# Attention's start in an adaptive-layer-norm block: modulation computed as rows, gates in their own buffers, the first stack signalled by heads

## The reference

```
mod = silu(c) @ wmod                      # c: 8 x 512, wmod: 512 x 3072
sa, ca, ga, sb, cb, gb = six slices of mod, 8 x 512 each
ga, gb = sign * max(|g|, 0.25)            # sign(0) counts as +1
h = layernorm(x) * (1 + ca) + sa
x = x + ga * attention(h)                 # 16 heads of 32, causal
h = layernorm(x) * (1 + cb) + sb
x = x + gb * ffn(h)                       # 512 -> 1024 -> 1024 -> 512, relu
```

## Time and profile before

| What | us |
|---|---|
| median of 3 runs | 1556.97 |
| lowest and highest run | 1556.32, 1560.2 |
| the profiled execution | 1558.07 |
| its span in the trace | 1556.3 |
| TensorE (PE) busy | 1454.3 (93%) |
| VectorE (DVE) busy | 1110.4 (71%) |
| ScalarE (ACT) busy | 808.8 (52%) |
| GpSimd (POOL) busy | 450.3 (29%) |
| mean granted clock of TensorE | 0.97 |

### The profile page before, as it was taken

One profiled execution on the slowest core, in us unless ns is written; L12 is line 12 of the kernel. 1 busy time (PEld: TensorE's weight loads), 2 busy tenths in 40 slices (PEclk: granted clock), 3 DMA queues, 4 the chain that ended last, 5 costly groups with the idle time before them and its releaser, 6 DMA issues.

```text
span 1556.3 us, 30453 instructions
## 1 busy us (share of the span) xinstructions
PE 1454.3 (93%) x12112; PEld 1319.0 (85%) x12112; DVE 1110.4 (71%) x1953; ACT 808.8 (52%) x1462; POOL 450.3 (29%) x455
## 2 busy tenths in 40 slices
PE   7989999999999999994699999987999999999998
PEld 6678788787878888873499999987999999999998
DVE  5477878777877777672676667676676665788887
ACT  3157666667666666673355555555333333354332
POOL 2156566656576766673000000020000000000000
PEclk9889999999999999996799999998999999999999
DMA  6534444343534343434334444642665555688885
GB/s 216 162 84 123 98 97 123 89 121 80 125 82 124 90 124 82 99 77 170 134 132 153 142 143 142 230 163 82 237 227 207 210 210 184 232 279 288 304 304 183
DMA packets 126590, 247.16 MB, mean 159 GB/s; under 512 B 13672, under 2 KB 36200, under 8 KB 126448
## 3 DMA queue, kind: packets, MB, share of 16 engines
q1 hardware_dynamic: 122816, 242.57, 49.7%
q10 hardware_dynamic: 3632, 2.64, 0.5%
HBM read 114.58 MB, written 79.72 MB: 125 GB/s over the span
## 4 chain that ended last, share of the span: by engine, by line
PE 45%; DVE 4%; ACT 2%; DMA 2%; issue 1%; SPq 0%; DVEq 0%; ACTq 0%
PE sum_b L2125 11%; PE sum_e L2125 8%; PE sum_a L2125 8%; PE aux L2065 6%; PE sum_b L2121 4%; PE sum_e L2121 3%; PE sum_a L2121 3%; PE aux L2075 1%; PE aux L2053 1%; DMA y_dram<-u_c 1%; DVE op L1708 1%; DVE w L1832 1%; DMA wproj_whole<-wproj_t 1%; DVE w L1837 0%; ACT w L1493 0%
## 5 line engine op out<-in xcount | busy, mean ns | idle before, releaser
L429 POOL TENSOR_TENSOR prob_lo<-prob,prob_hi 128x512 f16<-128x512 f32 x256 | 297.2, 1166 | 138.3 <-ACT prob L533 138.0
L526 ACT ACTIVATE prob_hi<-key_score 128x512 f16<-128x512 f32 x320 | 191.2, 598 | 127.7 <-PE key_score L824 125.2
L2125 PE MATMUL sum_b<-op,w 128*128 128x256 f32 x1728 | 221.8, 287 | 12.0 <-DVE op L1708 9.7
L2125 PEld LDWEIGHTS sum_b<-op,w 128*128 128x128 f32 x1728 | 215.0, 195 | 14.8 <-DVE op L1708 7.2
L735 PE MATMUL lin<-h_parts,wqkv 128*128 128x512 f32 x768 | 218.5, 408 | 1.1 <-DVE h_parts L578 1.1
L533 ACT ACTIVATE prob<-key_score 128x512 f32<-128x512 f32 x320 | 190.6, 596 | 0.0
L697 DVE TENSOR_REDUCE row_max<-score 128x1 f32<-128x512 f32 (+2 forms) x384 | 180.4, 498 | 12.8 <-PE score L811 11.9
L735 PEld LDWEIGHTS lin<-h_parts,wqkv 128*128 128x128 f32 x768 | 143.0, 195 | 30.4 <-DVE h_parts L578 3.2
L2125 PE MATMUL sum_e<-op,w 128*128 128x256 f32 x1152 | 151.1, 289 | 5.4 <-DVE w L1832 5.4
L811 PE MATMUL score<-stack 96*128 96x512 f32 (+3 forms) x512 | 155.2, 364 | 0.0
L2125 PEld LDWEIGHTS sum_e<-op,w 128*128 128x128 f32 x1152 | 146.2, 197 | 6.4 <-DVE w L1832 5.8
(11 more groups left out here) (153 smaller groups left out, 2583.5 us busy)
## 6 DMA issues: line engine op xcount, KB each, us to landing
stack<-qk_parts SPq DMA_DIRECT2D x384, 128.0 KB, 2.4
late_op_whole<-y_dram SPq DMA_DIRECT2D x40, 512.0 KB, 4.9
y_dram<-u_c SPq DMA_DIRECT2D x32, 512.0 KB, 3.1
blk<-y_dram SPq DMA_DIRECT2D x32, 512.0 KB, 4.3
y_dram<-y_sum SPq DMA_DIRECT2D x24, 512.0 KB, 4.4
x_tiles<-x SPq DMA_DIRECT2D x32, 256.0 KB, 3.7
attn_dram<-o_rows SPq DMA_DIRECT2D x32, 256.0 KB, 2.3
attn_tiles<-attn_dram SPq DMA_DIRECT2D x8, 1024.0 KB, 6.3
```

Of the source, the lines that this page charges most:

```text
L429: nc.gpsimd.tensor_tensor(prob_lo[:, key[1] % 2, u, :], prob[:, u, :], prob_hi[:, key[1] % 2, u, :], ALU.subtract).then_inc(lo_pool, 1)
L526: nc.scalar.activation(prob_hi[:, q % 2, u, :], bank[:], ACT.Exp, scale=SOFTMAX_SCALE, bias=P_SHIFT)
L2125: mm = nc.tensor.matmul(dst, w[:, wl, c, cols], data[:, dl, c, :], start=begin, stop=end, skip_group_check=again)
```

## The change

It does the following.

- Modulation: `mod_columns(s)` no longer computes, it transposes. New `mod_row_of(s, j)` computes one of the four vectors as rows (8 x 512) by four float32 matmuls like a gate's; ACT copies the row to the new tile `mod_rows` (`take_row`), and TensorE transposes it in four pieces of 128 into `o_bank`. The two vectors of attention come ahead of the turns, their transposes after turn 1. The MLP's two are computed in slot 0, steps 1 and 3, and transposed in slot 1, step 4.
- Ahead of it TensorE runs 16 bf16 matmuls of 128x512 of the identity (`warm_up`), as soon as POOL has made identity and masks.
- Turns 2 and 3 of batch 0 use the two score banks, and `o` instead of `full`; QK 0 and QK 1 of batch 0 are interleaved piece by piece. The weights' high and low parts are put later, one piece at a time, the last two low parts into slot 0.
- Gates: they are computed in slot 1, step 2, and slot 2, step 2, with a weight tile of their own (`wm_gate`); ACT copies each to `gates`, POOL makes each by four instructions ahead of its slots 2 and 3, and SP stores them ahead of slot 3. `gates` and `sign` now share memory with stack 3, so that stack's load and its ones wait for the store; DVE's `take_gate` is gone.
- Stack 0 of batch 0 is loaded head by head, three DMAs a head, with a semaphore for each head; slots 0 and 1 wait for the head that they need.

```diff
     def load_mod(engine, i):
...
+        dst, arrived = (wm[:, half], wm_in[half]) if i < 4 else (wm_gate[:], wm_gate_in)
+        engine.dma_start(dst, wmod.rearrange("(c p) n -> p c n", p=P)[:, :, column * C:(column + 1) * C])\
+            .then_inc(arrived, 16)
+    def turn_bank_of(n, c):
+        return score_bank[c - 2] if n == 0 and c >= 2 else lin_bank_of((TURN, c))
+    def full_of(n, c):
+        return o[:, c - 2].rearrange("p t n -> p (t n)") if n == 0 and c >= 2 else full[:, c % 2, :]
...
# SP
+                if n == 0 and g == 0:
+                    sp.sem_inc(stack_in[0], 16 * STACK_DMAS)
                     for j in range(4):
+                        for block_row in range(3):
+                            load_rows(g, block_row, j, first_stack_in[j])
+                    return
+                if n == 0 and g == 3:
+                    sp.wait_ge(gates_out, 16)
+                for block_row in range(3):
+                    for j in range(4):
+                        load_rows(g, block_row, j, stack_in[g])
...
-            for step in (1, 2):
-                sp.wait_ge(mod_mm, step)
-                for half in range(2):
-                    load_mod(sp, 2 * step + half)
-                for item in before_first():
-                    if item[0] == QK and item[1] // 2 == step - 1:
-                        after_item(0, item)
+            for half in range(2):
+                sp.wait_ge(mod_mm, half + 1)
+                load_mod(sp, 2 + half)
+            load_mod(sp, 4)
+            for item in before_first():
+                after_item(0, item)
...
-                    if first and (p, u) == (1, 3):
+                    if first and (p, u) == (3, 0):
                         sp.wait_ge(gate_step, GATE_STEPS)
# POOL
+            def make_gate(g):
+                made = 4 * g
+                pool.wait_ge(gate_row, g + 1)
+                nc.gpsimd.tensor_scalar(sign[:, g], gates[:, g], 0.0, 0.5, ALU.is_ge, ALU.subtract)\
+                    .then_inc(gate_step, 1)
+                pool.wait_ge(gate_step, made + 1)
+                nc.gpsimd.tensor_tensor(gates[:, g], gates[:, g], sign[:, g], ALU.mult).then_inc(gate_step, 1)
+                pool.wait_ge(gate_step, made + 2)
+                nc.gpsimd.tensor_scalar(gates[:, g], gates[:, g], GATE_FLOOR / 2, 4.0, ALU.max, ALU.mult)\
+                    .then_inc(gate_step, 1)
+                pool.wait_ge(gate_step, made + 3)
+                nc.gpsimd.tensor_tensor(gates[:, g], gates[:, g], sign[:, g], ALU.mult).then_inc(gate_step, 1)
...
             def slot(b, p, first, more):
+                if first and p == 1:
+                    pool.wait_ge(w_lo, len(W_ORDER))
+                    pool.wait_ge(v_split, values_until(1))
+                    ones(2)
+                    pool.wait_ge(ones_ready, 4)
+                if first and p in (2, 3):
+                    make_gate(p - 2)
+                if first and p == 4:
+                    pool.wait_ge(mod_mm, 6)
+                    pool.wait_ge(gates_out, 16)
+                    pool.wait_ge(v_split, values_until(4))
+                    pool.wait_ge(lo_pool, 3 * len(LO_ON_POOL))
+                    ones(3)
+                    pool.wait_ge(ones_ready, 1 + GROUPS)
# ACT
+            def take_row(s, j):
+                act.wait_ge(mod_mm, 2 * s + j + 1)
+                nc.scalar.copy(mod_rows[:, s, j], key_bank[j][0:B, :]).then_inc(mod_row, 1)
+            def take_gate(g):
+                act.wait_ge(mod_mm, 4 + g + 1)
+                act.wait_ge(w_lo, len(W_ORDER))
+                nc.scalar.copy(gates[:, g], (key_bank[0], o_bank)[g][0:B, :]).then_inc(gate_row, 1)
+            for j in range(2):
+                take_row(0, j)
+            weights_high(0)
             for item in before_first():
                 after_item(0, item, very_first=True)
+                if item == (TURN, 1):
+                    weights_high(1)
                 if item == (TURN, NC_ - 1):
+                    weights_high(2)
+                if item == (QK, 1, NC_ - 1):
                     for k in range(3, len(W_ORDER)):
                         weights_high(k)
...
                 if first and p == 2:
-                    act.wait_ge(gates_out, 16)
+                    act.wait_ge(mod_turned, 2)
                 for u in range(UNITS):
+                    if first and p == 0 and u in (2, 4):
+                        take_row(1, u // 2 - 1)
+                    if first and (p, u) == (1, 2):
+                        take_gate(0)
+                        load_mod(act, 5)
+                    if first and (p, u) == (2, 3):
+                        take_gate(1)
# DVE
-            for k in range(3):
-                weights_low(k)
             take_columns(0)
             dve.wait_ge(mod_taken, 2)
             take_mod(0)
+            weights_low(0)
             for item in before_first():
                 after_item(0, item)
-                if item == (TURN, NC_ - 1):
-                    for k in range(3, len(W_ORDER)):
-                        weights_low(k)
-            take_columns(1)
+                if item == (TURN, 1):
+                    weights_low(1)
+                if item == (QK, 1, NC_ - 1):
+                    weights_low(2)
+            weights_low(3)
...
-                    if first and p == 1 and u in (0, 2):
-                        take_gate(u // 2)
+                    if first and p == 0 and u in (1, 3):
+                        weights_low(4 + u // 2)
+                    if first and (p, u) == (2, 0):
+                        take_columns(1)
# TensorE
+            def warm_up():
+                for _ in range(WARM_UP):
+                    nc.tensor.matmul(score_bank[0][:], ident_bf[:], ident_bf[:].unsqueeze(1).broadcast_to([P, NT, P]),
+                                     start=True, stop=True)
+            def condition_row(bank, weights):
+                for c in range(NC_):
+                    mm = nc.tensor.matmul(bank[0:B, :], silu[:, c, :], weights[:, c, :],
+                                          start=(c == 0), stop=(c == NC_ - 1))
+                mm.then_inc(mod_mm, 1)
+            def mod_row_of(s, j):
+                pe.wait_ge(wm_in[j], 16 * (s + 1))
+                if s:
+                    pe.wait_ge(mod_row, j + 1)
+                condition_row(key_bank[j], wm[:, j])
             def mod_columns(s):
                 for j in (SHIFT, SCALE):
+                    pe.wait_ge(mod_row, 2 * s + j + 1)
                     for block in range(NC_):
                         at = ((s * 2 + j) * NC_ + block) * B
+                        mm = nc.tensor.transpose(o_bank[:, at:at + B], mod_rows[:, s, j, block * P:(block + 1) * P],
+                                                 ident[0:B, 0:B])
+                mm.then_inc(mod_turned, 1)
...
+            pe.wait_ge(pool_step, 8)
+            warm_up()
             pe.wait_ge(silu_step, 3)
+            for j in (SHIFT, SCALE):
+                mod_row_of(0, j)
+            first_items = before_first()
+            first_items[NC_:3 * NC_] = [item for pair in zip(qk(0), qk(1)) for item in pair]
+            for item in first_items:
                 do_item(0, item)
+                if item == (TURN, 1):
+                    mod_columns(0)
...
+                if b == 0 and p < 2 and u in (0, 2):
+                    pe.wait_ge(first_stack_in[2 * p + u // 2], 16 * 3)
...
                 if first and p == 2:
+                    pe.wait_ge(gate_row, 1)
+                    pe.wait_ge(ones_ready, 3)
+                if first and p == 3:
+                    pe.wait_ge(gate_row, 2)
+                if first and p == 6:
                     pe.wait_ge(ones_ready, 1 + GROUPS)
                 for u in range(UNITS):
+                    if first and p == 0 and u in (1, 3):
+                        mod_row_of(1, u // 2)
+                    if first and (p, u) == (1, 2):
+                        gate_row_of(0)
+                    if first and (p, u) == (1, 4):
+                        mod_columns(1)
+                    if first and (p, u) == (2, 2):
+                        gate_row_of(1)
```

113 lines of the change are left out of this document (48 added, 65 removed).

## The result

| What | before | after |
|---|---|---|
| median of 12 runs, us | 1560.66 | 1548.63 |
| lowest and highest run | 1556.32, 1565.1 | 1546.48, 1554.56 |
| the profiled execution | 1558.07 | 1547.02 |
| its span | 1556.3 | 1545.2 |
| POOL busy | 450.3 | 465.3 |

The ratio of the runs is 0.9931 with a 95% interval of 0.9915 to 0.9946: 12 us faster, where 18.2 were forecast, and 0.13 us outside the stated range, which is less than two repeats of the same kernel differ by (1548.76 and 1548.46). Up to 75 us the times came out nearly as predicted. Slot 4 then lost 4.5 us, in the step whose cost the prediction had put at 0.5.

The account below looks back on a forecast made before the run. TensorE was taken as always busy from the fourth slot, so earlier starts reach the end whole: 17.1 before slot 0 + 1.6 in slots 0 to 2 − 0.5 for gates = 18.2 off 1558.1, stated 1540.0 us; range 1534.5 to 1548.5.

Parts of the forecast that it names:

- What bounds it: TensorE is always busy from the fourth slot, so whatever attention ends earlier should reach the end whole.
- the first row: Start up to modulation's rows: warm-up, rows and transposes let DVE take the columns at 18.7 us, 4.0 earlier.
- QK 0 and 1: Batch 0's first QK matmuls: start at 22.7 us instead of 28.41, end at 30.3 with the clock fallen for part.
- Slots 0 to 2: Attention's first three slots: 13.4, 11.5 and 11.9 us, in all 36.8 instead of 38.4, so 1.6 earlier.
- The stack by heads: Stack 0's first head lands at 36.3 us, 1.8 to spare before slot 0; all twelve signalled at once, at 42.
- Gates on POOL: Four POOL instructions a gate, 1.2 to 4.7 us, fit ahead of slots 2 and 3; cost 0 to 2, taken 0.5.
- (B): Earlier start partly lost again in slots 0 to 4; gain 6 to 13 us, about 1548; chance 0.15.
- (A): Warm-up doesn't help, clock not up when rows start; 5.5 us of gain lost, 1545.5 us; chance 0.13.
- (C): No gain, within 0.3% (4.7 us), from a fixed bound after slot 3; 1556 us; chance 0.04.
- (D): Slower: SP stands at slot 3 on the gate steps, and stack 3 behind it; 1563 us; chance 0.03.
- (E): The clock also holds in QK and after; gain 21 us or more, 1536 us; chance 0.10.
- the signs that were to show the prediction wrong: Slot 3 early but the load not, granted clock falling between 40 and 90 us, or TensorE waiting for a stack.

Follow-up runs that it names:

- c1: Changed kernel with POOL's memset of stack 3's ones set ahead of slot 5 instead of slot 4; median 1548.29 us.
- a2: Changed kernel with gate 1's four POOL instructions left out, so the second gate is stored unmade; median 1545.35 us.
- b1: Changed kernel with both gates made by DVE, each in one piece after its first step of slots 2 and 3; median 1548.19 us.
- d3: Changed kernel with gate 0 by POOL in slot 1, gate 1 by DVE stepwise in slot 3, stack 3's ones ahead of slot 5; median 1545.16 us.
- c2: Changed kernel with gate 1's POOL instructions left out and stack 3's ones set ahead of slot 5; median 1544.61 us.
- b2: Changed kernel without the warm-up matmuls ahead of modulation's first row (WARM_UP = 0); median 1551.32 us.
- a0: The changed kernel run again unaltered, as yardstick of its set; median 1548.76 us.
- a3: Changed kernel with both gates on POOL, one instruction a step in slots 2 and 3, stack 3's ones ahead of slot 5; median 1547.72 us.

## Why the prediction was wrong, point by point

**What bounds it, the first row, QK 0 and 1: right.** Warm-up from 2.8 to 7.9 (8 to 9 predicted), rows at 8.97 and 13.17 (9.2 and 13.0), columns at 18.4 (18.7), QK from 22.2 to 29.8 (22.7 to 30.3), with the clock fallen from 23.0 to 26.4, 3.4 us where 4.9 were assumed. The eight tiny transposes, for which the prediction had no row, took 0.66 us (0.8).

**Slots 0 to 2: right in the sum, partly by luck.** Slot 0 is at 37.55 (38.1), slot 3 at 75.02 (75). But slot 1 takes 10.7 us (11.5 predicted) and slot 2 13.35 (11.9): TensorE has 12.4 us of work in it, and waits 0.9 for the maxima to land in the stack, which the prediction did not have. The misses cancel. In the two repeats slot 3 is at 76.0 and 75.1; a fall of the clock in slot 2 makes the first. Slot 1 waits for no row maximum, as predicted. The transfers that were doubted came in time: no wait of TensorE in slots 0 to 4 ends in one by SP, and stack 3's load is issued from 85.42 to 93.1.

**The stack by heads: right in its time, undersized in its worth.** The whole stack came at 41.0. What its absence costs is not the wait of 3.6 us but 5.1 by the start of slot 1, since the clock fell behind it.

**"Gates on POOL": this step failed.** It said that gate 1 fits ahead of slot 3's low parts and "Cost 0 to 2 us; I take 0.5". With the memset it cost 4.5 in slots 3 and 4. Three things were wrong in it. The size: 1.93 us for an instruction with one input and 1.27 for one with two make 6.4 us a gate, where 4.7 was taken as the upper bound. The bound from the nearest row was no bound, since the rows compared were of another kind of instruction. The cover: slot 3's row was read (4.82 us busy of 10.26) and slot 4's was not. Slot 4 has 9.18 of 11.76. The sum over both is 4.8 + 9.2 + 6.4 + 1.8 = 22.2 us of POOL work for 22.0 us of TensorE, where slot 3 alone, 4.8 + 4.7, seemed to leave room. The memset had been seen ("comes on top in slot 4") and not added up. And what is late next: the low parts behind gate 1, `full`, which POOL frees for the turns, and DVE's normalisation weren't named.

The last of the three weighs most, because the sum over both slots is a warning and not the cause. With the assumed 4.7 us a gate it would have read 20.5, below 22.0. c1 has 20.4 us of POOL work by it and loses the whole 4.5; a2 has 15.8 and loses 1.5. What the runs show in place of the step is a matter of order: 6.4 us in one piece delay every low part behind them, and TensorE waits for those by DVE's row maximum or by the turns. How the loss divides between these two ways stays open.

**The skill's rule.** That elementwise work belongs on VectorE was set aside since "by either figure the sum stays". The trace of after shows POOL at 1.27 us against DVE's 0.68 for the product of the same shape, which agrees with the rule's factor of two. For one input, with two operations in the instruction, the traces show 1.93 on POOL against 0.41 and 0.81 on DVE, where the same section of the Trainium skill's GPSIMD Engine Reference, When to use GPSIMD, has GpSimd at about line rate. There page and trace differ, and the trace decides. But moving the gates to DVE in one piece, as the rule would have it, gave nothing that the runs can tell (b1, 1.4 us lower, by -2.4 to 5.1): DVE is what TensorE waits for in slot 3. In d3, with gate 1 one instruction a step on DVE, slot 3 is whole; d3 also has gate 0 in slot 1 and the ones late, so its time isn't the order's alone.

**The sum.** 18.2 us were forecast; slot 5 starts 14.1 us earlier, and without the two pieces 18.8 (c2). The rest, from 14.1 at slot 5 to 12.0 in the medians, is traced to no part of the change and stays open. From slot 5's start to the end the changed kernel takes 1443.7, 1446.9 and 1443.8 us in three profiles; the kernel before takes 1440.7, and with the added POOL work 1444.7 and 1446.6. So before's one profile may have had a short tail by chance. It was 2.6 us under its later median of 1560.66; the sum was made against it (without taking off the 1.1 us that it names). Of the 8.6 us between 1540.0 and 1548.63, 2.5 are the starting point (1558.2 against 1560.7), 4.1 are lost by slot 5, nearly all of it in the gate step, and 2.0 lie behind slot 5. Without any cost of the gates the forecast would have read 1560.7 - 18.7 = 1542.0; c2, which comes nearest to that, has 1544.6.

**Rivals.** (B), part of the gain lost again in slots 0 to 4, among them "POOL's lateness, another fall of the clock", at about 1548 and a chance of 0.15, is what happened. That it hit the time to 0.6 us is luck: it meant a gain of 10 us from 1558, and the gain was 12.0 from 1560.7. Its chance was too small, since POOL's load in slot 4 had not been read. (A) is refuted by the rows of 3.6 us each and by b2, (C) and (D) by the result; SP's wait for the gates, (D)'s place, delayed nothing. (E), the clock holding in QK, didn't come in any profile. Two of the signs that were to show the prediction wrong came near: the granted clock fell at 91.2, where 40 to 90 had been named (and in a0 at 62.5), and TensorE waited 0.9 us for a stack.

## What to carry to other kernels

When work is moved to an engine "with room", add up that engine's busy time over every stage until the queue has drained, not over the stage where the work is put; add each small piece that the same change leaves there. A sum that doesn't fit is a warning, but one that fits is no proof: c1 fitted by 1.6 us and lost all the same. So follow, one by one, the instructions that stand behind the new piece, and name what their results free or feed, since those waits take the place of the one removed. Where several engines are nearly full, try such work as single instructions between the ones that are waited for: in slot 3, four in one piece cost DVE 4.5 us and TensorE a wait of 2.0, the same four by step 2.6 and no wait. It isn't a rule for every engine: the same cut on POOL (a3) only moved the loss into slot 3.
